# A transformer block on one core: the low-order weight product of the expert stage in half-height matmuls

## The reference, cut to what matters

```
xf = x.reshape(-1, x.shape[-1])
router_logits = jnp.einsum('th,eh->te', xf, Wr)
topk_vals, topk_idx = jax.lax.top_k(router_logits, TOP_K)
h = jnp.einsum('th,efh->etf', xf, Wi) + bi[:, None, :]
h = jax.nn.gelu(h, approximate=False)
expert_out = jnp.einsum('etf,ehf->eth', h, Wo) + bo[:, None, :]
```

## Time and profile before

| | before |
|---|---|
| time, median of 3 runs | 643.41 us |
| span of the profiled execution, first to last instruction | 639.0 us |
| what lies around the span (643.41 - 639.0) | 4.4 us |
| PE busy in the span | 578.6 us, 91% |
| DVE, ACT, POOL busy | 421.9, 334.7, 272.3 us |
| expert stage | about 328 us to the end |
| granted TensorE clock, mean | 0.977 |

### The profile page before, as it was taken

The page is one execution under the profiler, slowest core; times in us unless marked ns, Lnnn a source line. Parts: engine busy times, 40 slices in busy tenths (PEclk is TensorE's granted clock), DMA queues, the critical chain, the costliest instruction groups (busy, mean ns, idle before and its releaser), DMA issues.

```text
span 639.0 us, 14571 instructions
## 1 busy us (share of the span) xinstructions
PE 578.6 (91%) x3844; PEld 543.2 (85%) x3845; DVE 421.9 (66%) x1549; ACT 334.7 (52%) x722; POOL 272.3 (43%) x314
## 2 busy tenths in 40 slices
PE   3999999889989989988658999999999999999992
PEld 3899887777878877777558999999999999999992
DVE  4678888677887887888885555555555555555650
ACT  1533234555656666555256555555555555555650
POOL 3322332015645645554652444444444444444442
PEclk9899999989999999999959999999999999999998
DMA  8960000401111111111241333333333333332221
GB/s 269 409 268 0 0 2 19 149 13 56 57 37 43 68 38 37 68 43 38 69 120 32 51 50 50 50 50 50 50 51 51 51 51 50 54 39 39 39 26 19
DMA packets 31827, 42.41 MB, mean 66 GB/s; under 512 B 4597, under 2 KB 27798, under 8 KB 31671
## 3 DMA queue, kind: packets, MB, share of 16 engines
q0 software_dynamic: 13488, 13.74, 13.9%
q1 hardware_dynamic: 18196, 28.19, 13.7%
q10 hardware_dynamic: 114, 0.15, 0.1%
HBM read 24.49 MB, written 17.57 MB: 66 GB/s over the span
## 4 chain that ended last, share of the span: by engine, by line
PE 37%; DMA 6%; DVE 3%; issue 3%; POOL 1%; POOLq 0%; ACT 0%; DVEq 0%; ACTq 0%
PE ps L1268 35%; DMA out_rows<-const,y_id 6%; PE ps L1273 1%; PE ps L1272 1%; POOL y_id L675 1%; DVE we_lo L1222 0%; POOL out_rows L679 0%; POOLq L204 0%; DVE over L1087 0%; DVE n_tiles L1089 0%; DVE const L1246 0%; ACT we_hi L814 0%; DVE table_parts L1092 0%; DVE const L1252 0%; DVE table_parts L1097 0%
## 5 line engine op out<-in xcount | busy, mean ns | idle before, releaser
L823 ACT ACTIVATE hT<-ps,b_i_sb 128x256 f32<-128x256 f32 (+1 forms) x240 | 95.0, 446 | 119.9 <-PE ps L1268 119.8
L1268 PE MATMUL ps<-w_o_sb,hT 128*128 x852 | 145.3, 327 | 0.9 <-DVE const L1246 0.9
L679 POOL DMA_INDIRECT out_rows<-const,y_id x71 | 123.2, 1736 | 42.0 <-POOL y_id L675 29.4
L1268 PEld LDWEIGHTS ps<-w_o_sb,hT 128*128 128x128 f32 x852 | 137.5, 191 | 1.2 <-issue 1.2
L1268 PE MATMUL ps<-n_hi,we_hi 128*128 128x256 f32 (+1 forms) x480 | 129.8, 293 | 4.4 <-DVE n_hi L1230 2.5
L1268 PEld LDWEIGHTS ps<-n_hi,we_hi 128*128 128x128 f32 x480 | 92.5, 193 | 5.4 <-DVE we_lo L1222 4.9
L1268 PE MATMUL ps<-n_hi,we_lo 128*128 128x256 f32 (+1 forms) x480 | 96.4, 283 | 0.0
L1222 DVE TENSOR_TENSOR we_lo<-we_all,we_hi 128x768 fp32r<-128x768 f32 x80 | 73.2, 957 | 22.0 <-issue 20.7
L1268 PEld LDWEIGHTS ps<-n_hi,we_lo 128*128 128x128 f32 x480 | 74.8, 193 | 0.0
L1268 PE MATMUL ps<-nA_lo,we_hi 128*128 128x256 f32 (+1 forms) x240 | 67.8, 283 | 0.0
L1246 DVE TENSOR_TENSOR const<-ps,b_o_sb 128x384 f32<-128x384 f32 (+1 forms) x40 | 20.5, 512 | 69.7 <-PE ps L1268 37.5
(11 more groups left out here) (235 smaller groups left out, 1168.7 us busy)
## 6 DMA issues: line engine op xcount, KB each, us to landing
we_all<-in_w_i SPq DMA_DIRECT2D x8, 768.0 KB, 13.6
conv_only<-lists SPq DMA_DIRECT2D x31, 194.0 KB, 2.9
w_o_sb<-in_w_o SPq DMA_DIRECT2D x8, 576.0 KB, 17.8
out_rows<-X SPq DMA_DIRECT2D x16, 192.0 KB, 1.9
X<-in_x SPq DMA_DIRECT2D x1, 1536.0 KB, 11.3
out_rows<-const,y_id POOLq DMA_INDIRECT x71, 3.6
conv_only<-lists SPq DMA_DIRECT2D x9, 97.0 KB, 2.5
we_all<-in_w_hid SPq DMA_DIRECT2D x1, 776.0 KB, 7.1
```

The costliest lines, as they stand in the source:

```text
L679: pool.indirect_dma_start(out=out, out_offset=bass.IndirectOffsetOnAxis(ap=y_id[:, odd, t:t + 1], axis=0), in_=y_sb[:, odd, t, :], in_offs ...
L823: last = act.activation(hT[:, odd, f, 0:n].unsqueeze(1), ps_h[:, b, c, 0:n].unsqueeze(1), ACT.Gelu, bias=b_i_sb[:, ds(e * FCHUNKS + f, 1)])
L1268: return pe.matmul(dst, lhsT, rhs, start=start, stop=stop)
```

## The change

The fourth matmul of a column block, `we_lo[b]` by `sB` over 128 partitions, is replaced. It held two products: the low weights by the high rows and the low weights by the low rows, which is the smallest of the four. The new one has only the first, over 64 partitions. Since the weights of the 64 channels lie twice in the partitions, the block with even f takes them from partitions 0 to 63 and the block with odd f from 64 to 127, and the rows have to be there twice too: the new tile `sB_two` takes the place of `sB` (high part above, low part below), and `sB_hi` holds the high part in all 128 partitions. ACT writes the upper half of `sB_two` in an additional copy. Both half-height matmuls come after the eight others of their two column blocks, and the blocks get a PSUM bank each (0, 1, 2, 4, 5, 6).

```
-        ps_h = ps[:, 0:FCHUNKS // 2, :].rearrange("p b (c n) -> p b c n", c=2)
+        ps_h = [ps[:, f + (f >= 3), 0:TWO] for f in range(FCHUNKS)]
...
-                    act.activation(sB[:, 0:n], ps_sT[:, 1, 0:n], ACT.Copy).then_inc(sT_hi_done, 1)
+                    act.activation(sB_two[0:KB, 0:n], ps_sT[0:KB, 1, 0:n], ACT.Copy)
+                    act.activation(sB_hi[:, 0:n], ps_sT[:, 1, 0:n], ACT.Copy).then_inc(sT_hi_done, 1)
...
-                    dve.tensor_tensor(sB[KB:P, 0:n * P], ps_sT[KB:P, 1, 0:n * P], sB[KB:P, 0:n * P].bitcast(f32),
+                    dve.tensor_tensor(sB_two[KB:P, 0:n * P], ps_sT[KB:P, 1, 0:n * P], sB_hi[KB:P, 0:n * P].bitcast(f32),
...
-                                 (we_hi[:, odd, b], sB[:, 0:n]), (we_lo[:, odd, b], sB[:, 0:n]),
-                                 (we_lo[:, odd, a], sA_hi[:, 0:n]))
+                                 (we_hi[:, odd, b], sB_two[:, 0:n]), (we_lo[:, odd, a], sA_hi[:, 0:n]))
                         for k, (w, x_part) in enumerate(pairs):
-                            last = mm(ps_h[:, f // 2, f % 2, 0:n], w, x_part, k == 0, k == len(pairs) - 1)
+                            mm(ps_h[f][:, 0:n], w, x_part, k == 0, False)
                         if f % 2:
+                            for g, rows in ((f - 1, slice(0, KB)), (f, slice(KB, P))):
+                                w = we_lo[rows, odd, FF + g * P:FF + (g + 1) * P]
+                                last = mm(ps_h[g][:, 0:n], w, sB_hi[rows, 0:n], False, True)
                             last.then_inc(h_ps, 1)
```

More of the change, by code:

```diff
@@ L265, in build @@
         nB_bias = sb("nB_bias", [KBB, SEQ], f32r)
+        sB_two = sb("sB_two", [P, TWO], f32r)
         zT, qT, kT = (xc[0:QK, :, :, :].rearrange("p a t c -> p (a t c)")[:, n * SEQ:(n + 1) * SEQ] for n in range(3))
@@ L356, in build @@
         meta = sb("meta", [P, MOE_TILES, 2, 2], i32)
-        sA_hi, sA_lo, sB = nA_hi, nA_lo, nB
+        sA_hi, sA_lo, sB_hi = nA_hi, nA_lo, nB
         y_at = CONST_AT["fwd0"][0]
@@ L822, in moe_step @@
                             f = 2 * b + c
-                            last = act.activation(hT[:, odd, f, 0:n].unsqueeze(1), ps_h[:, b, c, 0:n].unsqueeze(1),
+                            last = act.activation(hT[:, odd, f, 0:n].unsqueeze(1), ps_h[f][:, 0:n].unsqueeze(1),
                                                   ACT.Gelu, bias=b_i_sb[:, ds(e * FCHUNKS + f, 1)])
```

## The result

The changed kernel takes 673.93 us, the median of four runs (670.78 to 676.26), against 644.32 us (642.64 to 645.30) for the kernel before: a ratio of 1.046 with an interval of 1.043 to 1.050, some 29.6 us slower. The forecast was 678.6 us in a range of 668 to 695, from two halves that run at once and two passages for each pair.

What follows compares the result with a forecast made beforehand. PE was taken to bound the expert stage. Passages 46.8 us, less 14.0 saved by overlap, plus 2.4 lag, make 35.2 us more: span 639.0 to 674.2, plus 4.4 around it, 678.6 us, range 668 to 695.

Steps and rivals of the forecast that it cites:

- The bound: Expert stage, pair and single tiles: PE sets the pace, so a microsecond of PE is a microsecond of the kernel.
- the uncovered copy: Single tiles: the additional ACT copy would show with 0.09 us a tile, 0.8 us in all; counted as covered.
- The passage: Array shape changes 128 to 64 rows and back around each pair: 0.39 us, times 120 pairs 46.8 us.
- The overlap: Both halves of a pair run at once on different array rows, saving one step each: 14.0 us; chance 0.50.
- two bounds: Saving from the half-height matmuls lies between 0 (no overlap) and 14.0 us (both halves at once).
- one half after the other: Rival: the second half's load waits for the first's, so halves gain nothing; 690.2 us, chance 0.38.
- the passages are not free: Denies the rival that passages are free with weights 64 high, only the saved step counting: 631.8 us, chance 0.05.
- the loads are not hidden: Denies the rival that only the engine's emptying shows, loads going ahead on free rows: 653.4 us, chance 0.04.
- third passage: Rival: each tile empties the engine, adding a passage between the halves, with no overlap: 714 us, chance 0.03.
- the estimate of 676.7 us: Alternative total from the skill page's 4 ns between row groups: lag 0.5 us in all in place of 2.4.
- The lag between halves: The second half of a pair starts slightly after the first: 0.02 us, times 120 pairs 2.4 us.
- The 4.4 us around the span: Time outside the profiled span, added to the 674.2 us span to give 678.6 us.

Runs made afterwards that it cites:

- e1: The changed kernel with the two half-height matmuls of a pair done over all 128 partitions again, copy, banks and order kept: 643.18 us, ratio 0.998 to the kernel before.
- e2: The changed kernel with both halves of a pair taking weights and rows from partitions 0 to 63: 688.6 us, ratio 1.065 to the kernel before.

## Why the prediction was right

*The bound* held in the pair tiles, where PE is the chain before and after, and the copy, the banks and DVE cost nothing in them (e1). In the single tiles the chain of the kernel before runs through POOL's writes of the output rows, from 575 us on, and only in the changed kernel through PE; that PE bounds them too rested on its 48.92 busy of 49 us, and the stage did grow by what its matmuls grew. There the additional copy may show when no passage covers it: a single tile takes 5.57 us in e1, against 5.49 before, close to the 0.09 that the prediction had priced for the uncovered copy.

*The passage.* The price of 0.39 us in and out, from another stage, another number of rows and plain `f32`, was met: 0.396 us between pairs of column blocks in the pair tiles of the changed kernel. That a price for 32 rows would do for 64 had no row to rest on, and that the two agree so closely is in part luck. The Trainium skill, "TensorEngine Tiling (Array Packing)", Tiling Modes, names the emptying at a change of mode; the trace agrees, with a load that begins 0.09 us late on the way in (507.26 in place of 507.05 + 0.118). It adds that, by the starts of the loads, the other half of the 0.39 us is two loads of 0.11 that no longer run beside a matmul.

*The overlap.* Taken as the likelier of two bounds without a row of its own, it holds: 14.7 us by e2 against 14.0 in the sum. Of the rivals, one half after the other is what e2 was built as, and it cost 688.6 us (forecast 690.2). The other rivals are refuted by the same rows: the passages are not free (0.396 us), the loads are not hidden, and between the halves there is no third passage (0.003 us between their loads). The page "TensorE: Matmul & The Clock Gate", Part 3, of the Trainium skill was the better guide here: by it loads and matmuls on different rows run together, and the estimate of 676.7 us worked out from it lies nearer.

*What was off* is the size, 35.2 us forecast for 29.6. Three terms were too large. The lag between halves, 2.4 us, is not there: two loads end within the length of one. In single tiles a pair costs 0.53 / 3 = 0.18 us net, so in and out is 0.18 + 0.11 = 0.29 in place of 0.39, 27 x 0.10 = 2.7 us, which is the amount that the text had left to the range. And the last pair of a pair tile pays 0.22 net in place of the forecast 0.39 - 0.118 = 0.27, 31 x 0.05 = 1.6 us, since its way out leads into the transposes, which the prediction had not told apart. The other 62 pairs pay 0.006 more than forecast, 0.4 us. Together 6.3 us too much, for the 5.6 between the forecast and the medians. The 4.4 us around the span are no error of this kind, but they are not what lies around it: executions with a span of 639.0 took 641.06 and 641.07 us, so 2.1 us do, and the rest is the spread of the runs. They stand on both sides of the sum and cancel.

## What to carry to other kernels

A matmul on half the array's rows pays for its passages only in runs: a passage into and out of the shape costs about three steps of a 256-column matmul here, a pair of halves saves one, and three pairs in one run are a draw. Look at the loads (PEld) for idle time where the number of rows of the array changes, whether the profile puts it down to "issue" or to nothing, measure it from starts, and count the changes before counting the saved matmuls. And before a stall is removed, ask who waits next: in attention the same 0.39 us was hidden behind DVE, and removing it gained nothing.

## What the runs showed of the hardware that was not expected

The price of a passage depends on what follows it: on the way out into a transpose of 128 columns it was 0.06 us lower than into a 256-column matmul, and the load of the transpose is 0.05 us shorter. Two weight loads on different rows of the array ran side by side, 0.003 us apart, and on the same rows one behind the other, 0.11 us apart. And taking work from an engine that is not the bound made the kernel slower: with 0.4 us more idle time an image, PE's granted clock was at its lower level in parts of attention (0.86 in five windows that had 1.00 before), for 9 us. What made it fall in these five images and not in the others is not shown.
